# An attention and mixture-of-experts block on one core: head loads set between stores, the token search cut into two halves with other matmuls between its own, and the expert loop written out

## The reference, cut to what matters

```python
h = _layernorm(x) * (1 + ca) + sa
x = x + ga * attention(h)            # scores: relu(q k) * R_hat(|i-j|), causal
h = _layernorm(x) * (1 + cb) + sb    # this is xf below, 4096 x 256
scores = softmax(xf @ gate_w.T)      # 4096 x 8
vals, idx = top_k(scores.T, 512)     # per expert: which tokens, what weight
y = layernorm(xf[idx]) * ln_w + ln_b
out = (gelu(y @ fc1 + b1) @ fc2 + b2) * vals
xf = xf.at[idx].add(out)
x = x + gb * xf
```

## Time and profile before

| | us |
|---|---|
| three runs, median | 1559.85 |
| lowest and highest of them | 1557.88, 1561.18 |
| the profiled execution, its time on the device | 1563.45 |
| its span, from first to last instruction | 1561.4 |
| TensorE busy in it | 1457.0 (93%) |
| VectorE busy | 1195.1 (77%) |
| ScalarE busy | 1063.5 (68%) |
| GpSimd busy | 928.1 (59%) |
| mean granted TensorE clock, 1 being 2.4 GHz | 0.96 |

### The profile page before, as it was taken

The page is one execution under the profiler, slowest core; times in us unless marked ns, Lnnn a source line. Parts: engine busy times, 40 slices in busy tenths (PEclk is TensorE's granted clock), DMA queues, the critical chain, the costliest instruction groups (busy, mean ns, idle before and its releaser), DMA issues. The chain is left out here.

```text
span 1561.4 us, 43682 instructions
## 1 busy us (share of the span) xinstructions
PE 1457.0 (93%) x16142; PEld 1139.9 (73%) x16142; DVE 1195.1 (77%) x3650; ACT 1063.5 (68%) x2293; POOL 928.1 (59%) x1542
## 2 busy tenths in 40 slices
PE   6994999999999999999999999999997648999997
PEld 4551788888888888888888888888876536666675
DVE  6643999999999999999999999999966694223222
ACT  3443788888888888988888888888874760211211
POOL 3332788778877877788777787788783002334322
PEclk9996899999999999999999999999998856999999
DMA  6334222322232223222232223222335324334431
GB/s 221 122 113 151 72 66 64 95 73 66 64 93 73 67 63 90 76 68 87 70 95 71 64 69 93 72 65 66 122 128 156 94 88 136 98 85 111 142 75 23
DMA packets 90031, 142.44 MB, mean 91 GB/s; under 512 B 18032, under 2 KB 69632, under 8 KB 85728
## 3 DMA queue, kind: packets, MB, share of 16 engines
q1 hardware_dynamic: 82058, 128.70, 26.6%
q0 software_dynamic: 6464, 9.29, 3.2%
q10 hardware_dynamic: 1302, 1.74, 0.3%
HBM read 109.56 MB, written 30.15 MB: 89 GB/s over the span
## 5 line engine op out<-in xcount | busy, mean ns | idle before, releaser
L804 PE MATMUL score_ps<-region_s 128*128 128x512 bf16 (+3 forms) x1280 | 405.3, 353 | 8.9 <-DVE maxima L883 4.6
L815 PE MATMUL turn_ps<-ident,region_a 128*128 128x128 f32 x2048 | 328.7, 274 | 2.8
L815 PE MATMUL turn_ps<-ident,region_x 128*128 128x128 f32 x2048 | 330.1, 274 | 0.0
L918 POOL TENSOR_SCALAR region_x<-region_x,maxima 128x1664 f32<-128x1664 f32 (+3 forms) x128 | 202.2, 1580 | 176.9 <-ACT region_x L855 173.5
L815 PEld LDWEIGHTS turn_ps<-ident,region_a 128*128 128x128 f32 x2048 | 255.2, 141 | 41.6 <-ACT region_c L850 10.1
L883 DVE CUSTOM_DVE_ANT_0 region_x<-score_ps,region_t,maxima 128x512 f32<-128x512 f32 (+1 forms) x416 | 268.9, 698 | 16.1 <-PE score_ps L804 16.1
L815 PEld LDWEIGHTS turn_ps<-ident,region_x 128*128 128x128 f32 x2048 | 253.0, 141 | 27.8 <-ACT region_o L850 6.5
L850 ACT ACTIVATE region_p<-turn_ps 128x512 f32<-128x512 f32 x384 | 223.9, 608 | 68.3 <-PE turn_ps L815 68.0
L850 ACT ACTIVATE region_o<-turn_ps 128x512 f32<-128x512 f32 x448 | 265.9, 616 | 0.2
L855 ACT ACTIVATE region_x<-region_x 128x384 f32<-128x384 f32 (+1 forms) x512 | 247.1, 507 | 3.9 <-DVE maxima L883 3.4
L883 DVE CUSTOM_DVE_ANT_0 region_a<-score_ps,region_t,maxima 128x512 f32<-128x512 f32 (+1 forms) x352 | 230.5, 693 | 17.3 <-PE score_ps L804 17.3
(11 more groups left out here) (218 smaller groups left out, 2420.1 us busy)
## 6 DMA issues: line engine op xcount, KB each, us to landing
region_t<-factor_rows SPq DMA_DIRECT2D x32, 1024.0 KB
region_x<-in_fc_t SPq DMA_DIRECT2D x16, 1024.0 KB, 8.5
region_s<-q_split SPq DMA_DIRECT2D x64, 192.0 KB
region_s<-k_split SPq DMA_DIRECT2D x64, 192.0 KB
q_split<-region_o SPq DMA_DIRECT2D x16, 384.0 KB, 2.7
k_split<-region_t SPq DMA_DIRECT2D x16, 384.0 KB, 2.6
heads_out<-region_o SPq DMA_DIRECT2D x254, 17.0 KB
region_x<-in_x SPq DMA_DIRECT2D x4, 1024.0 KB, 15.3
```

The lines of the kernel that those rows point to most:

```text
L804: nc.tensor.matmul(score_ps[:, j % SB, 0:(hi - lo) * P], stacks[:, b, 0, t * P:(t + 1) * P], stacks[:, b, 1, lo * P:hi * P], start=True, s ...
L815: last = nc.tensor.transpose(turn_ps[:, (h * NR + j) % TB, q * P:(q + 1) * P], rows[t][:, k * P:(k + 1) * P], ident[:, :])
L918: nc.gpsimd.tensor_scalar(row, row, maxima[:, 4, n:n + 1], 1.0, ALU.add, ALU.mult).then_inc(shifted_pool, 1)
```

## The change: what it does

Three things are changed.

**The loads of head 0.** `load_head` becomes a sequence of seven calls of `load_part`. In the projection block the first of them, the factor load, now stands behind the store of unit 20, and the six others one behind each of the stores of units 21 to 26. The wait for batch 0's stores moves from ahead of unit 24 to ahead of unit 20.

**The search.** The one-hots are laid out by halves of the experts, and formed, multiplied and turned into token numbers half by half (`a` = 0, 1). Five base pairs stand between the finds of the first half, one behind every six finds, and six between those of the second, one behind every four. VectorE's adds of the first five pairs move from behind all one-hots to between those of the second half. The first half's token numbers are spread behind four finds of the second, the second half's behind the turn of expert 0's tokens. That turn now waits for each of its four fetches apart. The two halves write to separate PSUM banks.

**The experts.** The loop is written out: constants stand where registers stood.

```diff
 def load_part(sp, h, b, m):
+    if m == 0:    # factor_rows -> factors[:, b, :]
+    elif m <= 3:  # q_split, part m-1, copied 3, 3, 2 times
+    else:         # k_split, first, count = ((0, 3), (3, 3), (6, 2))[m - 4]
...
-                    if u == 4 * (NG // B) + 2 * SPLITS:
+                    if u == 4 * (NG // B) + SPLITS:
                         for i in range(SPLITS):
                             sp.wait_ge(st_split[i], 16 * 4 * (NG // B) // SPLITS)
                         sp.wait_ge(st_dist, 64)
-                        load_head(sp, 0, 0)
                     sp.wait_ge(part3, u + 1)
                     sp.dma_start(dst[...], parts[u % SPLITS]).then_inc(st_split[u % SPLITS], 16)
+                    part = u - 4 * (NG // B) - SPLITS
+                    if 0 <= part < HEAD_LOADS:
+                        load_part(sp, 0, 0, part)
...
-            pe.wait_ge(onehot_done, 3)
-            for a in range(E // QE):
-                for t in range(NT):
-                    c = t * (E // QE) + a
-                    last = nc.tensor.matmul(found_ps[:, a, :], low_hot[:, :, :, c]..., token_of[:, :, :, :, c]...)
-                last.then_inc(tokens_mm, 1)
-            pe.wait_ge(tokens_done, 1)
-            for q in range(QE):
-                last = nc.tensor.matmul(spread_ps[:, q, :, :], spread_ident[:, q, :, :]..., idx_f[:, :, q, :])
-            last.then_inc(idx_spread, 1)
-            for p in range(PB, PAIRS):
-                gate_pair(p)
+            pe.wait_ge(onehot_done[0], 3)
+            pair = PB
+            for t in range(NT):
+                find(0, t)
+                if t % 6 == 5:
+                    gate_pair(pair)
+                    pair += 1
+            pe.wait_ge(onehot_done[1], 3)
+            for t in range(NT):
+                if t == 4:
+                    spread_indices(0)
+                find(1, t)
+                if t >= 8 and t % 4 == 0:
+                    gate_pair(pair)
+                    pair += 1
...
             pe.wait_ge(base_done, PAIRS)
-            turn(0, 0)
-            over_experts(pe, emit)
+            turn_first()
+            spread_indices(1)
+            for e in range(E):
+                expert(e)
...
+            high_ones(0)
+            with_tiles(0)
+            low_ones(0, 0, LOW)
+            add_base(0)
+            high_ones(1)
+            add_base(1)
+            with_tiles(1)
+            add_base(2)
+            low_ones(1, 0, LOW // 2)
+            add_base(3)
+            low_ones(1, LOW // 2, LOW)
+            add_base(4)
...
+            indices(0)
+            add_base(PB)
+            save_indices(0)
+            for p in range(PB + 1, PAIRS):
+                add_base(p)
+            indices(1)
             normed_in(0, 0)
-            over_experts(dve, emit)
+            save_indices(1)
+            for e in range(E):
+                expert(e)
```

176 lines of the change are left out of this document (105 added, 71 removed).

## The result

The changed kernel took 1552.52 us (median of five runs, 1548.45 to 1553.16), the kernel before on the same chip 1559.98 (five runs, 1557.88 to 1562.74). The ratio is 0.9945, with a 95% interval from 0.9928 to 0.9962. The median lies 0.5 us above the upper end of my range (1538.5 to 1552). That range was worked out from a kernel before of 1559.85; the ratio times 1559.85 is 1551.3, just inside it. Both are far from the forecast of 1544.0. The profiled execution took 1552.23 us with a span of 1550.0, against 1563.45 and 1561.4.

The account below looks back on a forecast made before the run. Chains of waits were taken as the bound: loads queued on few DMA engines, then VectorE and TensorE taking turns in the search. Gains of 8.5 + 7.4 + 0 = 15.9 us off 1559.85 gave 1544.0, range 1538.5 to 1552.

Parts of the forecast that it names:

- Part 1: Projection block: spacing head 0's loads between stores removes ScalarE's 18.00 us wait, ending split(31) at 129.8, not 138.29; gain 8.5 us.
- the loads hide wholly: Rival, projection block: the DMA engines' queue is no limit and TensorE sets the end; 16.5 instead of 8.5, time 1536, chance 0.06.
- the stores pay in full: Rival, projection block: each store behind a load takes 2.6 us instead of 1.2, no gain from loads; time 1553.7, chance 0.07.
- Part 2: Mixture block's search: one-hots by halves with base pairs between finds end the first fc1 at 1333.0, not 1340.39; gain 7.4 us.
- the find at the high clock: Search, second half: a find was taken to cost 0.17 us once the clock has risen, instead of 0.252.
- The rival in which the clock stays low: Search: the clock stays at 1.2 GHz through both halves, gain there 0; time 1551.4, chance 0.17.
- a high clock from the first find on: Rival, search: 2.4 GHz throughout, gain there 18.1 us; time 1533.3, chance 0.04.
- Part 3: Loop over the experts: writing it out is worth 0, since TensorE's chain has no gap at a loop turn.

Follow-up runs that it names:

- b3_rows: The changed kernel with each q and k load of head 0, batch 0 cut into one DMA a copy, 16 rows outermost; ratio 0.9850.
- c5_side_by_side: The changed kernel with the one-hots laid out so that what one find reads is adjacent in SBUF; 1576.78 us in one run.
- a2_search_written: The changed kernel with the loads of before, in one piece ahead of the store of unit 24; ratio 0.9952.
- b2_pairs_behind: The changed kernel with base pairs 5 to 15 behind all finds, as in the kernel before; ratio 0.9928.
- b1_filled: The changed kernel with seven matmuls of no use on TensorE ahead of the first find; ratio 0.9896.
- c3: The changed kernel with q and k loads taken apart by rows, seven unused matmuls ahead of the finds, expert 1's fetches behind the adds; ratio 0.9845, 1538.3 us.
- c4: The changed kernel with seven unused matmuls ahead of the finds and expert 1's fetches issued only after all base pairs are added; ratio 0.9895, 1545.88 us.
- d1_rows_later: The changed kernel with q and k loads taken apart by rows and expert 1's fetches behind the adds, no filling matmuls; ratio 0.9885.
- a3_written: The kernel before with its loop over the experts written out and nothing else; ratio 0.9989.

## Why the prediction was right, and where not

**Part 1, 8.5 us.** Mechanism and size hold. Forecast were `split(31)` at 129.8 and the attention block from 136.7; measured are 129.44 and 136.35, with six waits of 0.9 to 2.5 us in place of the one. That it fits to 0.4 us is luck, since two errors offset each other. By my count the store of unit 22, and with it `split(26)`, was due at 109.8 (101.5 + 3.1 + 1.2 + 2.8 + 1.2); it came at 112.45, of which 1.1 us is that the stage began later (unit 20's store issued at 100.06, not 98.93). The five steps behind it took 17.0 us, 3.4 each, and not 20.0. From `split(20)` on the gain is 9.9 us, 50.4 to 40.4. The rival that the loads hide wholly falls, as does the one in which the stores pay in full. b3_rows shows that the limit was the one named, a queue on two or three engines: with the same bytes over more engines 6.6 of the remaining 40.4 us went.

**Part 2, 7.4 us.** The stage was forecast at 54.5 us (1278.48 to 1333.0) and took 55.7 and, in the second profile, 55.6 (by the same ends). Right in it: one-hots of 0.10 us (3.28 for 32), the first find 6.3 us after the first high one-hot (6.0), the first half in 16.6 us at clock 0.5 (16.7), the clock's rise in the second of the six pairs, 0.89 a pair after it, the turn without a wait. The term that was mis-sized is the find at the high clock: I took 0.17, "since weight load and matmul both shrink", and it took 0.245. Nineteen of them stand behind the rise (I had 16 on either side of it), so this alone is 1.4 us. That the whole came out 1.2 over is the sum of several: the first find 0.3 late, the first half 0.1 short, from there to the turn 0.5 over (the 1.4, less cheaper spreads, 1.55 for 1.92, a pair of 1.48 for 1.7 in which the clock rose, and three finds that I had counted at 0.252), the step from turn to fc1 2.66 for 2.36, with the second spreads in it, and an fc1 of 13.97 for 13.73. c5_side_by_side shows why the find did not shrink: its price is the distance of its operands' elements in SBUF, not the clock. The rival in which the clock stays low falls by the windows, that of a high clock from the first find on is not this kernel, though b3_rows came near it.

**The figure that it was set against** failed more. I took 1340.39 of one profile as the kernel before, late adds included. The second profile has C at 56.5 instead of 61.7. Against it the change brings 1.1 us in this stage. I had also read the wait wrongly: VectorE was not behind, the increments of `base_mm` that it waited for came late. Of the 7.4 forecast some 5 rest on that one execution. Yet a2_search_written, timed over seven runs, gives 7.5 (4.9 to 10.4), more than 1.1. If the late adds are in most of the timed runs of before, the two agree; if they belong to the profiled executions, most of those 7.5 us have no place in any profile. Which of the two holds was not measured. What the profiles do show is small: the first find comes 2.7 us sooner (6.3 for 9.0 us after the first high one-hot), and the mixing gives most of that back (b2_pairs_behind). That the changed order makes late adds rarer is not shown: the search by halves has them in a2, b1, b2 and b3 and not in the changed kernel's own two profiles, c3, c4, c5 and d1. In a2 they cost under 1 us (C of 56.4).

**Part 3, 0.** Held: 28.42 us from fc1 to fc1 in both, and a3_written at 0.9989. The stall at a taken branch that the Trainium skill's page "Runtime: NRT & Kernel Launch" (Instruction fetch mechanics) describes is not seen here. It is said to come where the target lies outside the instructions held; whether this loop's does, no run shows.

**The sum.** 15.9 forecast; by times 7.5 in the first comparison and 14.0 in the second (1562.65 to 1548.63). The first time, set against 1559.85 by its ratio, is 1551.3 and looks like the rival of the low clock (1551.4), which the windows refute; that the range reached so far was for that rival, and the mechanism of the forecast does not give this number. The second, 0.9905, gives 1545.0, near the 1544.0. By profiles 11.4 and 13.7, where the edited stages have 15.0 and 11.3. The difference is made by stretches that nothing touches: B differs from 106.5 to 110.9 over fourteen profiles, the attention block from 1026.2 to 1031.1. "What lies outside is not touched, so I take the difference from the median" may be true of the mean, but not of one profile and hardly of five runs. The theory that the gain is given back in B falls in its plain form, since a3_written has 110.7 with the loads and the search of before. B's mean is 107.8 over the four profiles with the old loads and 109.1 over the ten with the new. Whether that 1.3 is more than chance, and why the first ratio came out so much nearer to 1 than the second, stays open.

## What to carry to other kernels

A stall that is read in one profile may not be there in the next: before it goes into a sum, a second profile of the same kernel is worth more than a third decimal. A DMA whose outermost dimension is two or three queues on two or three engines; moving it here took 10 us off the stage and left 13 us of waits, taking it apart by rows removed all but 1.7 of those. A matmul between far-apart elements did not shrink with the clock, so ask what the operands' step is before halving its price. And where an engine seems to hold another up, look first at whether the event that released it came on time, and whether the trace has all its events.

## What the runs showed of the hardware that was not expected

- A 128x128 bf16 matmul with its weight load took 0.24 to 0.25 us at both clocks with operand elements 128 and 512 bytes apart, 0.105 and 0.055 with adjacent ones.
- VectorE's comparison with a destination step of 256 bytes took 0.28 us (9.07 / 32) instead of 0.10, its product into the same layout 9.2 us instead of 1.22.
- In seven of fourteen profiles TensorE's semaphore increments reached VectorE late, by up to 3.5 us in b3_rows, and the same seven traces lack the landings of DMAs in that stage.
- With the same instructions on TensorE, the clock rose from 1.2 to 2.4 GHz at the second of the mixed pairs in one execution (b3_rows) and only in the second half of the search in another (d1_rows_later). Seven matmuls in the gap ahead of the finds kept it at 2.4 GHz in two of three profiles for the whole search, and for most of it in the third (b1_filled).
- The median of the kernel before differed from one comparison to another by up to 8.6 us (1559.98 and 1568.6), and on one chip by 4.8 (1568.6 and 1563.76). The change brought 7.5 and 14.0.
